# Expert mixture on one core: combining rows gathered from the highest expert down, the first column fetched during the expert loop, and codes sorted inside the loop

## The reference, cut to what matters

```python
scores = jax.nn.softmax(x2d @ wg_router.T, axis=-1)
topk_w, topk_idx = jax.lax.top_k(scores, TOP_K)                  # TOP_K = 6, E = 32
topk_w = topk_w / (jnp.sum(topk_w, axis=-1, keepdims=True) + 1e-20)
...
C = CAP_FACTOR * (T * TOP_K // E)                                # 384
valid = pos_in_e < C
safe_pos = jnp.where(valid, pos_in_e, 0)
...
ye = jnp.einsum('ecf,efd->ecd', jax.nn.silu(g) * u, w_down)
y_tok = ye[flat_idx, safe_pos] * vmask
y = jnp.sum(y_tok.reshape(T, TOP_K, D) * topk_w[..., None], axis=1)
sh = jax.nn.silu(x2d @ ws_gate) * (x2d @ ws_up) @ ws_down
return y + sh
```

```python
x = x + 0.5 * _L0_ffn_ref(_layernorm(x), ...)      # stage 0, moe0
x = x + _L0_attn_ref(_layernorm(x), ...)           # stage 1, ret
x = x + 0.5 * _L0_ffn_ref(_layernorm(x), ...)      # stage 2, moe0
x = x + 0.5 * _L1_ffn_ref(_layernorm(x), ...)      # stage 3, bin
...                                                # stages 4 to 11
```

## Time and profile before

| what | value |
|---|---|
| time, median of 3 runs | 1925.78 us (1925.01 to 1929.13) |
| profiled execution, from its first to its last instruction | 1930.3 us |
| PE, DVE, ACT, POOL busy | 1682.2, 1476.8, 1188.9, 868.8 us |
| mean granted TensorE clock | 0.924 of full speed |
| indirect gathers on POOL: token rows `work<-Hd` | 128, 123.4 us |
| indirect gathers on POOL: result rows `ering<-ye` | 96, 94.1 us |

### The profile page before, as it was taken

One profiled execution on the slowest core, in us unless ns is written; L12 is line 12 of the kernel. 1 busy time (PEld: TensorE's weight loads), 2 busy tenths in 40 slices (PEclk: granted clock), 3 DMA queues, 4 the chain that ended last, 5 costly groups with the idle time before them and its releaser, 6 DMA issues. The chain is left out here.

```text
span 1930.3 us, 29481 instructions
## 1 busy us (share of the span) xinstructions
PE 1682.2 (87%) x10866; PEld 1371.6 (71%) x10866; DVE 1476.8 (77%) x3059; ACT 1188.9 (62%) x2391; POOL 868.8 (45%) x854
## 2 busy tenths in 40 slices
PE   6899579978995567798879998889999999998899
PEld 4799247857993345696669787667777777776688
DVE  7888677667886677687778666788888888889666
ACT  4588246645881169416841543888888888888443
POOL 0775432105765500301531210267878878778411
PEclk9899779989997589798979998999999999999799
DMA  8797212315983200000010010000000100100111
GB/s 307 225 290 245 71 53 90 117 38 180 288 264 99 84 1 2 1 1 0 1 59 39 27 41 1 21 8 28 23 23 23 33 15 21 33 1 14 53 41 36
DMA packets 74605, 139.86 MB, mean 72 GB/s; under 512 B 11476, under 2 KB 52564, under 8 KB 73428
## 3 DMA queue, kind: packets, MB, share of 16 engines
q1 hardware_dynamic: 63700, 108.50, 17.2%
q0 software_dynamic: 10752, 29.37, 5.2%
HBM read 113.73 MB, written 24.12 MB: 71 GB/s over the span
## 5 line engine op out<-in xcount | busy, mean ns | idle before, releaser
L79 PE MATMUL ps<-H_r,wt_r 128*128 128x512 f32 (+1 forms) x732 | 287.1, 430 | 14.2 <-POOL wt_r L91 7.5
L91 DVE TENSOR_TENSOR work<-work,ps 128x512 f32<-128x512 f32 (+4 forms) x306 | 172.1, 562 | 108.3 <-ACT work L87 59.0
L79 PE MATMUL ps<-work_r 128*128 128x256 f32 (+2 forms) x1200 | 243.8, 294 | 6.5 <-DVE work_r L91 2.4
L87 ACT ACTIVATE work<-ps 128x512 f32<-128x512 f32 (+3 forms) x355 | 168.2, 496 | 127.3 <-PE ps L79 107.9
L79 PE MATMUL ps<-wt,work 128*128 128x256 f32 (+2 forms) x1144 | 224.8, 368 | 8.7 <-ACT work L87 5.9
L79 PEld LDWEIGHTS ps<-work_r 128*128 128x128 f32 (+1 forms) x1200 | 190.4, 188 | 20.8 <-DVE work_r L91 11.3
L79 PEld LDWEIGHTS ps<-wt,work 128*128 128x128 f32 (+1 forms) x1144 | 174.5, 199 | 37.9 <-ACT work L87 9.1
L79 PE MATMUL ps<-ering_r,work_r 128*128 128x256 f32 (+1 forms) x814 | 199.9, 314 | 0.4 <-ACT work L87 0.4
L99 DVE SCALAR_TENSOR_TENSOR wt<-ps,wt 128x511 f32<-128x511 f32 (+2 forms) x234 | 174.2, 747 | 22.9 <-ACT wt L87 17.2
L79 PEld LDWEIGHTS ps<-H_r,wt_r 128*128 128x128 f32 (+1 forms) x732 | 140.3, 192 | 71.3 <-issue 12.9
L87 ACT ACT_TABLE_LOAD x113 | 145.0, 1283 | 46.8 <-DVE lmv L119 28.3
(11 more groups left out here) (248 smaller groups left out, 4204.8 us busy)
## 6 DMA issues: line engine op xcount, KB each, us to landing
ering<-in_moe_w SPq DMA_DIRECT2D x87, 624.0 KB, 5.7
ye<-work SPq DMA_DIRECT2D x64, 256.0 KB, 5.1
wt<-in_ssd_wg SPq DMA_DIRECT2D x64, 128.0 KB, 2.2
ye<-early SPq DMA_DIRECT2D x1, 4096.0 KB, 14.5
wt<-in_ssd_wg SPq DMA_DIRECT2D x8, 512.0 KB, 3.6
Hd<-H SPq DMA_DIRECT2D x16, 128.0 KB, 1.7
wt<-in_ret_fc SPq DMA_DIRECT2D x2, 1024.0 KB, 12.2
work<-Hd,work POOLq DMA_INDIRECT x128, 4.2
```

The costliest lines, as they stand in the source:

```text
L79: self.last = self.e.matmul(o, l, r, start=start, stop=stop, skip_group_check=True)
L87: self.last = self.e.activation(o, a, f, **kw)
L91: self.last = self.e.tensor_tensor(o, a, b, op)
```

## The change

1. **Order of columns.** The six columns of a tile are fetched and added in the order 5, 4, 3, 2, 1, 0, that is from the lowest expert of a token up to its highest, in both stages and all eight tiles.
2. **Column 5 in the loop.** A token has six different experts, so the lowest of them is at most 26. Column 5 of all eight tiles is gathered by a new `g_first` into `H` (not into the ring of nine buffers), for tiles 0 and 1 in step `in 30`, for tiles 2 to 7 in step `in 31`. It waits for the rows of experts 25 and 26. `g_combine` gathers five columns for a tile; column `i` waits for the rows of experts `30 - i` and `31 - i` only, and PE's product of expert 28 (the last whose weights lie under the nine buffers).
3. **Codes.** Segment 9 is a single multiplication, segment 10 has the sort, one subtraction and the conversion to `get`. A token that was not kept has its code clamped in segment 8 (its weight is zero) in place of being masked. The exact row numbers of `puts` are now made by `v_puts`, inside the branch that an overflow takes. The two instructions that set the flag `over` stand at the end of segment 8.
4. **Codes moved.** Segments 9 and 10 leave the place ahead of the loop and run in steps `in 0` and `in 1`: of both halves in stage 0, of the second half in stage 2 (where the first half is routed during `ret`).

```diff
-            todo.append(("half", si, 1, 9))
             todo.append(("slots", si))
             todo.append(("up", 33, 0))
-            todo.append(("half", si, 1, 10))
-            if si == 0:
-                todo += [("half", si, 0, seg) for seg in (9, 10)]
...
             def expert(e):
-                for seg in ("in", "mid", "out"):
-                    todo.append((seg, e))
-                    if seg != "out":
-                        yield
+                todo.append(("in", e))
+                if e < 2:
+                    todo.extend(("half", si, h, 9 + e) for h in ((1,) if si else (0, 1)))
+                elif e == 30:
+                    todo.extend(("early", si, t) for t in range(2))
+                elif e == 31:
+                    todo.extend(("early", si, t) for t in range(2, NT))
+                yield
+                todo.append(("mid", e))
+                yield
+                todo.append(("out", e))
...
-                v.tt(r.code, pos, bc(ecap[:, 0:32].unsqueeze(1), [128, n, 32]), ALU.add).then_inc(V)
+                v.stt(r.code, pos, CAP - 0.75, bc(ecap[:, 0:32].unsqueeze(1), [128, n, 32]), ALU.min, ALU.add).then_inc(V)
...
             elif seg == 9:
                 v.wait_ge(V)
-                v.tt(r.codes, r.code, r.keep, ALU.mult).then_inc(V)
-                v.wait_ge(V)
-                v.tt(r.codes, r.codes, drop, ALU.add).then_inc(V)
-                v.wait_ge(V)
-                v.tt(r.codes, r.codes, r.sel, ALU.mult).then_inc(V)
+                v.tt(r.codes, r.code, r.sel, ALU.mult).then_inc(V)
...
-                v.wait_ge(V)
-                v.copy(M0.puts[:, cs, :], r.pf).then_inc(V, "put", si, h)
-                v.ts(r.pf, r.pf, float(SLOTS - 1), ALU.min).then_inc(V)
...
+        def rows_stored(g, si, last):
+
+            for e in (last - 1, last):
+                g.wait_ge(s_ye[e % 2], "out", si, e)
+
+        def g_first(g, si, t):
+            g.wait_ge(V, "get", si, t // HALF)
+            g.wait_ge(s_yfill, "in")
+            g.wait_ge(s_rows, "out", si)
+            rows_stored(g, si, 26)
+            g.gather(H[:, t, :], None, ye[0:27 * CAP, :], get[:, t, 5:6]).then_inc(s_first[t], "in", si, t, by=16)
+
         def g_combine(g, si, t):
-            for i in range(6):
-                k = 6 * t + i
-                g.wait_ge(V, "get", si, t // HALF)
-                g.wait_ge(s_yfill, "in")
-                for j in range(2):
-                    g.wait_ge(s_ye[j], "out", si, 30 + j)
-                g.wait_ge(PE, "experts", si)
+            for i in COLUMNS[1:]:
+                k = 5 * t + 4 - i
+                rows_stored(g, si, 31 - i)
+                g.wait_ge(PE, "out", si, 28)
                 if k >= NGB:
-                    g.wait_ge(V, "gathered", si, (k - NGB) // 6, (k - NGB) % 6)
-                g.gather(gb[k % NGB], None, ye, get[:, t, i:i + 1]).then_inc(s_gb[k % NGB], "in", si, t, i, by=16)
+                    g.wait_ge(V, "gathered", si, (k - NGB) // 5, 4 - (k - NGB) % 5)
+                g.gather(gb[k % NGB], None, ye[0:(32 - i) * CAP, :], get[:, t, i:i + 1]).then_inc(s_gb[k % NGB], "in", si, t, i, by=16)
```

More of the change, by code:

```diff
@@ L660, in build @@
         s_gb = [sig(f"gather{i}") for i in range(NGB)]
+        s_first = [sig(f"first_gather{t}") for t in range(NT)]
         gb = [ering.rearrange("p a b -> p (a b)")[:, i * 256:(i + 1) * 256] for i in range(NGB)]
@@ L927, in v_add @@
         def v_add(v, si, t, i):
-            v.wait_ge(s_gb[(6 * t + i) % NGB], "in", si, t, i)
             v.wait_ge(V, "wk", si, t // HALF)
-            if i:
-                v.wait_ge(V, "gathered", si, t, i - 1)
-            else:
-                v.wait_ge(V, "shared", si, 33, t)
-            v.stt(X[:, t, :], gb[(6 * t + i) % NGB], wk[:, t, i:i + 1], X[:, t, :], ALU.mult, ALU.add)
+            if i == 5:
+                row = H[:, t, :]
+                v.wait_ge(s_first[t], "in", si, t)
+                v.wait_ge(V, "shared", si, 33, t)
+            else:
+                k = 5 * t + 4 - i
+                row = gb[k % NGB]
+                v.wait_ge(s_gb[k % NGB], "in", si, t, i)
+                v.wait_ge(V, "gathered", si, t, i + 1)
@@ L964, in v_step @@
             elif s[0] == "combine" and s[2] > 1:
-                for i in range(6):
+                for i in COLUMNS:
                     v_add(v, *s[1:], i)
@@ L995, in g_overflow @@
             o = OV[si]
-            for h in range(2):
-                g.wait_ge(V, "put", si, h)
             g.wait_ge(V, "over", si)
@@ L1322, in g_moe0 @@
                     g.wait_ge(s_join, "in", si)
+                elif s[0] == "early":
+                    g_first(g, *s[1:])
                 elif s[0] == "fetch":
```

48 lines of the change are left out of this document (39 added, 9 removed).

## The result

The changed kernel takes 1916.6 us (median of four runs, 1915.6 to 1921.9) against 1926.2 beside it: a ratio of 0.9944, interval 0.9929 to 0.9960. It is faster, by 9.6 us where 11.0 were forecast. Its profiled execution has a span of 1920.1 us against 1930.3.

| stretch | before, ends at | after, ends at | difference | forecast |
| --- | --- | --- | --- | --- |
| start of the kernel to the last expert of the first loop | 187.01 | 187.19 | +0.2 | -1.0 |
| to the end of the first mixture | 217.81 | 219.55 | +1.6 | 0 |
| `ret` | 419.14 | 419.22 | -1.7 | -0.3 |
| to the last expert of the second loop | 579.21 | 580.44 | +1.2 | 0 |
| to the first weights of `bin` | 609.43 | 607.17 | -3.5 | -2.1 |

The account below looks back on a forecast made before the run. POOL's issuing of gathers was taken as the bound behind the second mixture. The terms 2.1 + 7.6 + 0 + 1.0 + 0 + 0.3 = 11.0 us, off 1925.8, gave 1914.8 us, range 1910.5 to 1920.8.

Parts of the forecast that it names:

- Column 5 in the loop: POOL, both loops: two gathers fit in idle time, six follow; POOL free at 196.2 and 588.4, other columns 1 us earlier.
- End of the second mixture: Behind the second loop: DVE's first add and gate product start earlier, so the stage ends 2.1 us earlier, bounds 0.5 to 3.6.
- `bin`: Result-row gathers behind the second mixture: 30 in place of 36, POOL still bound by 1.4 us; 7.6 us gained, bounds 6.0 to 8.9.
- Codes moved, first loop: Start of the first loop: sums begin sooner, loop 1.0 us earlier; bounds 1.7 us lost to 2.4 gained.
- a wait of PE in the first loop that wasn't there: Sign named in advance that the prediction is wrong: a new PE wait in the first loop; no size given.
- Second loop: Start of the second loop: the one moved half is covered by DVE's waits for ACT; 0, bounds -0.6 to +0.5 us.
- End of `ret`: Last tile of `ret`: a subtraction and a conversion leave DVE's way; 0.3 us gained.
- 1, slow early gathers: Both loops: all eight early gathers take 1.75 us each, so the 2.1 us fall away; 1916.9 us, chance 0.06.
- 2, DVE the next bound: In `bin`: DVE's waits for ACT and PE replace those for gathers, half of 7.6 us lost; 1918.6 us, chance 0.12.
- 3, the loop pays for the codes: First loop: `in 0` is held by something else than the sums, 1.7 us lost, not 1.0 won; 1917.5 us, chance 0.14.
- 4: Both mixtures: column 5's eight gathers wait for the loop's end, ahead of column 4; 5.2 us slower, 1931, chance 0.04.
- 5: In `bin`: transfers set the pace, not POOL's issuing, so 30 gathers take as long as 36; 1922.4 us, chance 0.05.

Follow-up runs that it names:

- first column late: The changed kernel with the eight gathers of column 5 issued only behind the loop, ahead of the others: 1932.3 us, ratio 1.0033 to the kernel before.
- six columns down: The changed kernel with all six columns gathered behind the loop from the highest expert down, none early: 1924.7 us, ratio 0.9992 to the kernel before.
- codes back: The changed kernel with segments 9 and 10, in shortened form, ahead of the loop again: 1921.8 us, ratio 0.9977 to the kernel before.
- Weights late: The changed kernel with SP loading weights of experts 3 and 6 only after expert 1's rows landed: 1916.3 us, again 1914.1; ratios 0.9923, 0.9925 to before.
- shorter block: The changed kernel without `v_puts` in the overflow branch that is jumped over: 1920.1 us, ratio 0.9941 to the kernel before.
- rows first: The changed kernel with expert 1's rows gathered right behind expert 0's, ahead of POOL's memset: 1921.4 us, ratio 0.9947 to the kernel before.

## Why the prediction was right, point by point

**Column 5 in the loop** was right in place and size: two gathers between the subtractions, six behind, POOL free at 196.26 where 196.2 was worked out. The first column late shows what this place is worth: with the same 30 gathers in `bin`, 13.0 us.

**End of the second mixture** gave 3.5 us, not 2.1. The term was made of one thing, the gate product's start, and that came 2.2 us earlier behind the last expert. The reason given was in part another: the prediction had column 5 in `H` free DVE's first add, but with six columns down, where column 5 lies in the ring like the others, the gate product comes as early. The order and its weaker waits are enough. The other 1.3 us are PE's 16 products (5.41 against 6.68). The prediction named them as what could change it and set its bound to 3.6 for it. With the change the stretch from the last expert to `bin` is 26.7 us where they take 5.41 us, and 27.4 with the weights late, where they take 6.1. Their length goes with the granted clock: 0.69 over the 5.41 us and 0.55 over the 6.68. The shorter length is in all three traces of the change, so it may belong to it (PE's pause ahead of the products fell from 6.72 to 4.49 us), but no run tests that. In the first mixture it fell the other way, which makes the +1.6 us in the table:

```profile
211.71 6.78 PE L79 MATMUL ps<-ering,wt 128*128 128x256 f32 x16 [9.43 <-DVE wt L91]
```

against 5.16 us, with the gate product at 210.24 and 210.12. Over these 6.78 us the granted clock was 0.54, and over the 5.16 before 0.72. `ret` was 1.7 us shorter, which in the sum roughly returns it, but nothing ties the two.

**`bin`** gave 7.5 us, 7.6 were forecast. That POOL would stay the bound by 1.4 us was wrong by about that amount: DVE waited only 0.33 us, and its own work from the first add of tile 2 (615.08) to the last was 31.9 us without that wait, where 30.7 were worked out. The two bounds were so near to each other that it made no difference to the sum.

**Codes moved, first loop**, is the term that was mis-sized: -1.0 forecast, +0.2 measured, and 0.6 to 0.8 us lost against the kernel with the codes back. The step that failed is "landing takes 2.8 us or more, so `in 1` cannot start before 59.2". That bound was true and useless: the rows took 6.0 us to be used. The prediction took it that the gather doesn't move, and didn't ask what the earlier sums set off: PE's third block of `up 33` ended 2.2 us earlier and with it released the load of expert 3's weights, which now goes out together with this gather (56.69 and 56.72; 58.93 and 56.41 before). Weights late shows that the loads are the cause: held back, the rows land 4.1 us after the gather and not 5.9. With `in 1` at 62.72 all that DVE won at expert 0 (58.92 against 62.42) ran into a wait of 2.77 us, and the sorts stood behind the wait instead of in it. Part came back later: the wait ahead of expert 5's weights, before the change 1.60 us,

```profile
81.99 0.93 DVE L91 TENSOR_TENSOR ering_r<-ering,work_r 128x736 fp32r<-128x736 f32 x1 [1.60 <-ACT work_r L87]
```

is 0.77 us in the changed kernel, as for any other expert, so that +0.9 us at expert 2 were +0.1 at expert 5. "What is gained or lost at expert 0 stays to its end" was therefore too simple. One of the signs of being wrong that the prediction named, a wait of PE in the first loop that wasn't there, was to be seen: the 4.58 us.

**Second loop**: 0 forecast, +1.2 measured, over the bound of 0.5. Of the cover that was named (1.17 and 1.05 us of waiting for ACT) the second was there, and the sort fit into it: from the low part of expert 1 to the gate product DVE took 2.40 us, and 2.34 before. The first was gone, since DVE itself was late: it had stood 4.99 us without a releaser ahead of expert 0. The prediction had no term for a stop behind the branch. The shorter block gave 0.4 to 1.1 us of this back; the later rows (`in 1` at 456.20, 455.58 before) are the likely rest.

**End of `ret`**, 0.3 us, can't be told from the 5 us by which the stage differs between traces.

**The rivals.** 1, slow early gathers: no, 0.94 to 0.96 us, and in each mixture one of 1.17 or 1.18. The Trainium skill, "SBUF — State Buffer", section "SBUF: two separate sides", has GpSimd blocked only beside certain operations of DVE, among them one with two inputs from SBUF. This trace agrees as far as it goes: the two slower gathers started 0.07 and 0.06 us into such a subtraction (48x256, at 191.27 and 584.53), the others did not start within one. The estimate of 25 us took every gather to be blocked. 2, DVE the next bound: it is, but it cost nothing of the 7.6 us. 3, the loop pays for the codes: half true, 1.2 us lost against the forecast in each loop, for other reasons than the ones given there (`in 0` did move, to 57.51). 4 was made by the experiment with the first column late, and came out at 5.7 us slower where 5.2 were worked out. 5 fell with the six columns down: 36 gathers and 30 differ by 8.7 us in the tail.

The sum fell short by 0.8 us in the spans: 1.2 and 1.2 lost in the loops, 1.3 won by PE's clock in the tail, and small pieces. That it came so near is in part luck: the gathers gave what was worked out, but the 2.4 us lost in the loops were half hidden by 1.3 us of a clock that no term had. The range has a slip of its own: 4.5 us gained with half a us added is 1921.8, and 1920.8 was written.

## What to carry to other kernels

When one engine issues a stream at a fixed pitch and another waits for it, count what can be issued in its idle time earlier; the pitch times the number moved is the gain, up to where the next engine binds. Before work is moved to where an engine "waits anyway", ask from which transfer that wait comes: the landing of a small gather was set by the large loads issued beside it. Ask, too, which transfers the work that you move sets off earlier: here the earlier sums released those loads. Holding them back by one wait gave more (4.2 us) than moving sorts around. In a loop where two engines run close to their limits, try the order over its whole length: the start may be 2.4 us better and the rhythm 0.2 us for every expert worse.

## What the runs showed of the hardware

- **Landing of an indirect gather.** 128 rows of 1 KB, issued in 0.95 us, landed 2.7 us later in the middle case where it fetched result rows behind the loop. At the start of a loop the second gather of expert 1 landed 3.9 us after its issue with the first load of 624 KB 2.5 us behind it (kernel before, first loop), 5.0 to 6.3 us with the load 0.04 us ahead of it to 0.7 us behind it, 7.6 us with the load 0.5 us ahead (codes back, second loop), and 3.3 to 4.6 us with the loads held back. No run here issues it much earlier than the loads.
- **DVE and POOL stand in each other's way in some phases only.** DVE's 128x736 subtraction, with two inputs from SBUF, delayed a gather's issue from 0.95 to 1.35 or 1.56 us; POOL's 128x512 subtraction delayed DVE's 48x256 one, 0.42 us long, to 0.87. In the usual rhythm 37 gathers beside the same instructions had a mean of 0.95 us: there the gather is the first to start, by 0.17 us. This agrees with the Trainium skill, "SBUF — State Buffer", "SBUF: two separate sides", in that the later one waits for the whole earlier one; the page gives a DVE operation with two SBUF inputs as a hindrance for a GpSimd operation that reads SBUF, and here it was one for a gather's issue too (which reads its row numbers from SBUF).
- **A stop of 2.8 to 6.4 us on DVE behind a branch that jumps ahead**, at the start of the second loop: 4.99, 4.12 and 5.18 us with the change, 5.11 with the codes back, 5.29 with six columns down, 4.81 with the first column late, 6.40 with the rows first, 3.12 and 2.84 with the weight loads held back, 4.29 and 4.36 with these held back and the rows first. With the shorter block DVE idles 1.49 us there and in the kernel before 2.02, both for ACT. The transfers of the changed kernel from 451 to 454 us, within the stop, have one packet of an instruction queue (packets, MB, share of 16 engines' time):

```profile
q8 instruction: 1, 0.02, 2.2%
```

  Such a packet lies within the stop of the kernels with the codes back (at 454.0 to 454.4) and with the weights late (444.6 to 445.0) as well. In the kernel before the same queue moved one at 449.8 to 450.2 and the next only at 456.2, outside DVE's wait. DVE may thus have waited for instructions, behind the loads; this is argued and not shown. The Trainium skill, "Runtime: NRT & Kernel Launch", section "Instruction fetch mechanics", says that a taken branch to a place that isn't yet loaded must wait for a transfer of it. The numbers fit that in part: a packet lies within every such stop, but DVE went on 0.6 us after it (weights late) to 4.6 us after it (rows first), and the trace doesn't tell whose queue it belongs to or what else DVE waited for.
